# Attention with expert dispatch on one core: row sums spread through a DRAM scratch, values turned by VectorE

## The chip, the core and the metric

The kernel runs on one core of a Trainium2 chip. A core has five engines with an instruction queue each: TensorE (PE, matrix products into PSUM), VectorE (DVE), ScalarE (ACT), GpSimd (POOL) and SyncE (SP, which here only issues DMAs). DMAs run on 16 DMA engines; SP, ScalarE and GpSimd each have a queue to them. Engines wait for each other by semaphores, and each does its own instructions in order. The metric is device time of one execution, in microseconds (us).

## What is computed

`x` and `ctx` are 16 × 256 × 512 numbers. The first half is attention over channels cut into heads, with `ctx` both as keys and as values; the second sends each of 4096 rows to 2 of 8 experts. The reference, cut:

```python
def _L0_xcond_ref(q, k, v, k_length):
    ...
    s = SCALE * jnp.log(k_length.astype(jnp.float32))[:, None, None, None]
    attn = jnp.einsum('bhdq,bhdk->bhqk', qh, kh)
    attn = jax.nn.softmax(s * attn, axis=-1)
    out = jnp.einsum('bhqk,bhdk->bhdq', attn, vh)
...
x = x + _L0_xcond_ref(_layernorm(x, axis=-1), ctx_2048, ctx_2048, itok_B_779_1933)
x = x + _L0_ffn_ref(_layernorm(x, axis=-1), L0_ffn_Wg, L0_ffn_w1, L0_ffn_w2)
```

There are 8 heads of 32 dimensions per batch entry, and 512 queries and 512 keys per head. The experts' layer takes a softmax over 8 logits, the top 2 with a capacity of 1280 rows per expert, two matrix products with a relu between, and adds the results with their gates.

## The kernel before

The function `attention_and_dispatch` makes the first half and writes rows for the experts; the rest of the program, the experts' two products, is not touched by the change.

Work goes by groups: a group is 128 rows of `x`, that is 4 heads × 32 dimensions, with 512 columns. There are 32 groups. A loop over **slots** s does in one slot the scores of group s, the exponentials and weighted sums of group s − 2 and s − 3, the division by the row sums of group s − 4, the logits of group s − 5, and the preparation of group s + 2. Each slot has four **steps** c = 0 to 3 (128 queries or keys each), and each step four **turns** i. The order of every engine is written out by hand in this loop; an edit at `(c, i) == (1, 1)` stands in turn 1 of step 1. Odd slots from 7 on also choose experts for a pair of groups (`pair_in`), which adds small VectorE instructions; GpSimd sends the chosen rows to DRAM in the slot after.

In one turn TensorE makes a score block (L1086, into one of three banks `ps_s`), of which VectorE takes the row maximum (L678), and a turned score block of an earlier group (L1037, into one of three banks `ps_t`) with the maximum subtracted inside the product, of which ScalarE takes the exponential (L460, into `probs`). At the end of a step TensorE adds the weighted sums of the values (L1007, into `ps_o`) and the row sums (L1013, into `ps_l`). Banks are handed out in the order of use: the table made by `bank_turns` numbers each use, and a use waits until the one three before it on the same ring is free (`s_bank`, `t_bank`).

Queries and keys are split into a high and a low part (`khi` by ScalarE at L452, `klo` by GpSimd at L406, `qhi`, `qlo`), and SP copies these into the stacks `kst` and `qst` two slots ahead (L291, L296). SP's order in a slot is: eight small transfers of the row maxima (L251), `xt` and `ct`, `xres`, the store of a result, three copies into `kst`, three into `qst`.

**Values.** The weighted sum needs the values with keys over partitions. TensorE turns `ct` by four transposes at turn 1 of step 2 (`values`, L1051, behind the four of `row_turned`, L1044), into a bank of `ps_t`; ScalarE copies the bank to `vt` (L467).

**Row sums.** `ps_l` holds each row sum in every partition of its head. ScalarE copies `ps_o` and `ps_l` at the end of step 0 (L475, L537) and loads one row per head into 64 partitions (`l_wide`, L541). VectorE takes the reciprocal there (L730) and splits it in two parts (L734, L736). ScalarE loads these as 8 rows (`r_rows`, L521), and TensorE spreads them over all partitions by a product with a 0/1 matrix into a bank of `ps_s` (`shares`, L1059, turn 1 of step 1). VectorE multiplies `o_sb` by that bank (L795); GpSimd adds `xres` (`residual`, L336), VectorE takes the statistics of the sum in step 3 (L695). The last three groups are divided in another way, without this path.

The stage ends with the last two groups and the dispatch of the last rows, and then the experts' products begin. Times in this text count from the first instruction.

## Time and profile before

| what | value |
|---|---|
| median of 3 runs | 2180.99 us (2179.78 to 2181.63) |
| profiled execution, its span | 2177.8 us |
| its granted TensorE clock, mean | 0.995 |
| TensorE busy | 2117.0 us, 97% |
| VectorE / ScalarE / GpSimd busy | 1008.1 / 712.9 / 470.4 us |
| stage of slots, 54 to 615 us: TensorE busy | 556.75 of 561 us |
| the same: VectorE, ScalarE, DMA share | 441.56 us, 358.73 us, 0.71 |
| end of the dispatch, 615 to 677 us: TensorE busy | 55.29 of 62 us |
| experts, 677 to 2177.8 us: TensorE busy | 1483.54 of 1500.8 us |

The profile is of one execution; the median of the runs lies 3.2 us above its span. A busy share is an average, and a matmul that is followed by a wait is drawn longer than it is, so a share near 1 does not tell that an engine never waited. The DMA share is the mean over 16 DMA engines.

### The profile page before, as it was taken

To read this page: it belongs to the slowest core of one execution; us is meant where nothing else is said; L and a number is where in the kernel's file an instruction comes from. 1 tells how busy PE (TensorE), PEld (TensorE's weight loads), DVE (VectorE), ACT (ScalarE), POOL (GpSimd) and SP (SyncE) were. 2 spreads that over 40 slices of the span, in tenths; PEclk is the share of its full clock that TensorE was granted. 3 is DMA by queue.
4 is the path that set the end of the run, shared out by engine and by line. 5 is a ranking of instruction groups with operands and counts; after the bars stand their busy time and mean duration, and the time that the engine had idled before them with its cause. 6 is when DMAs were issued, how large, how long until landed. Compare 5 with 4: busy or idle time off the path is not lost. (4 is left out here: it accounts for less than half of the span.)

```text
span 2177.8 us, 27085 instructions
## 1 busy us (share of the span) xinstructions
PE 2117.0 (97%) x10179; PEld 1518.8 (70%) x10179; DVE 1008.1 (46%) x1908; ACT 712.9 (33%) x1216; POOL 470.4 (22%) x593
## 2 busy tenths in 40 slices
PE   3999999999999999999999999999999999999997
PEld 1445454455547888878888887888888788888776
DVE  5677878878765434234324423423432342343211
ACT  1666666666652222113212212311311231132110
POOL 3334444343422111110301201031030102101101
PEclk9999999999999999999999999999999999999999
DMA  9876767776635435212613612422441252241101
GB/s 147 160 165 157 181 157 188 168 187 162 146 114 161 115 70 132 58 22 85 131 20 78 150 26 58 125 50 43 114 98 25 56 134 52 48 125 31 16 6 20
DMA packets 183895, 216.61 MB, mean 99 GB/s; under 512 B 39731, under 2 KB 111419, under 8 KB 183740
## 3 DMA queue, kind: packets, MB, share of 16 engines
q1 hardware_dynamic: 154128, 173.21, 34.1%
q0 software_dynamic: 22240, 37.92, 9.1%
q10 hardware_dynamic: 7372, 3.42, 0.7%
q8 instruction: 97, 1.59, 0.3%
q14 instruction: 58, 0.48, 0.1%
HBM read 113.93 MB, written 68.29 MB: 84 GB/s over the span
## 5 line engine op out<-in xcount | busy, mean ns | idle before, releaser
L1590 DVE SCALAR_TENSOR_TENSOR hlo<-ps_h,hhi 128x512 fp32r<-128x512 f32 x256 | 177.0, 692 | 928.4 <-ACT hhi L1467 928.4
L1467 ACT ACTIVATE hhi<-ps_h 128x512 fp32r<-128x512 f32 x256 | 152.9, 597 | 1123.4 <-PE ps_h L1731 1123.4
L1729 PE MATMUL ps_h<-xhi,w1hi 128*128 128x512 f32 x1024 | 404.9, 395 | 2.5 <-PEq L1316 1.3
L1748 PE MATMUL ps_y<-w2hi,hhi 128*128 128x512 f32 x1024 | 404.7, 395 | 0.7 <-DVE hlo L1590 0.7
L1749 PE MATMUL ps_y<-w2lo,hhi 128*128 128x512 f32 x1024 | 403.0, 394 | 1.0 <-issue 1.0
L1750 PE MATMUL ps_y<-w2hi,hlo 128*128 128x512 f32 x1024 | 403.7, 394 | 0.0
L1731 PE MATMUL ps_h<-xhi,w1lo 128*128 128x512 f32 x1024 | 403.6, 394 | 0.0
L1730 PE MATMUL ps_h<-xlo,w1hi 128*128 128x512 f32 x1024 | 403.0, 394 | 0.0
L678 DVE TENSOR_REDUCE nmax<-ps_s 128x1 f32<-128x512 f32 x512 | 335.7, 681 | 128.5 <-PE ps_s L1086 124.6
L460 ACT ACTIVATE probs<-ps_t 128x512 f32<-128x512 f32 x504 | 273.0, 604 | 183.1 <-PE ps_t L1037 145.8
L1729 PEld LDWEIGHTS ps_h<-xhi,w1hi 128*128 128x128 f32 x1024 | 192.3, 188 | 48.5 <-issue 3.9
L1749 PEld LDWEIGHTS ps_y<-w2lo,hhi 128*128 128x128 f32 x1024 | 193.1, 189 | 46.7 <-issue 1.5
L1730 PEld LDWEIGHTS ps_h<-xlo,w1hi 128*128 128x128 f32 x1024 | 193.0, 188 | 45.2
L1748 PEld LDWEIGHTS ps_y<-w2hi,hhi 128*128 128x128 f32 x1024 | 192.3, 188 | 46.0 <-DVE hlo L1590 1.1
L1731 PEld LDWEIGHTS ps_h<-xhi,w1lo 128*128 128x128 f32 x1024 | 192.3, 188 | 45.8
L1750 PEld LDWEIGHTS ps_y<-w2hi,hlo 128*128 128x128 f32 x1024 | 192.3, 188 | 45.8
L1086 PE MATMUL ps_s<-kst,qst 96*128 96x512 f32 x416 | 192.0, 472 | 30.5 <-DMA qst<-qlo 27.6
L1402 POOL DMA_INDIRECT out_x<-y,ids x64 | 103.3, 1614 | 453.6 <-DVE y L1632 439.0
L1086 PEld LDWEIGHTS ps_s<-kst,qst 96*128 96x128 f32 x416 | 81.7, 197 | 146.8 <-DVE nmax L678 76.7
L1037 PE MATMUL ps_t<-qst,kst 98*128 98x512 f32 x408 | 164.0, 406 | 1.9 <-DMA qst<-nturn 1.2
L1384 POOL TENSOR_TENSOR ids<-xtail,zeros 128x4 int32<-128x4 int32 x15 | 4.9, 328 | 712.8 <-DMA xtail<-dispatched 712.8
L1007 PE MATMUL ps_o<-probs,vt 128*32 128x512 f32 x1016 | 137.1, 612 | 3.3 <-ACT probs L460 3.3
(202 smaller groups left out, 2007.2 us busy)
## 6 DMA issues: line engine op xcount, KB each, us to landing
raw<-in_L_ffn_w SPq DMA_DIRECT2D x128, 512.0 KB, 4.9
qst<-qhi SPq DMA_DIRECT2D x64, 256.0 KB, 5.8
xin<-dispatched SPq DMA_DIRECT2D x60, 256.0 KB, 5.8
kst<-khi SPq DMA_DIRECT2D x52, 256.0 KB, 6.4
xt<-in_x SPq DMA_DIRECT2D x32, 256.0 KB, 3.1
ct<-in_ctx SPq DMA_DIRECT2D x32, 256.0 KB, 4.5
qst<-qlo SPq DMA_DIRECT2D x32, 256.0 KB, 6.8
xres<-in_x SPq DMA_DIRECT2D x32, 256.0 KB, 4.7
```

The lines of the kernel that those rows point to most:

```text
L460: nc.scalar.activation(probs[n % 3][:, i, :], t_at(k)[:], ACT.Exp).then_inc(t_free, 1)
L678: nc.vector.tensor_reduce(nmax[s % 2][:, i, c:c + 1], s_at(k)[:], AX, ALU.max, negate=True).then_inc(s_free, 1)
L1037: nc.tensor.matmul(bank[:], kst[g % KR][0:STACK + 2, i, cols], qst[g % KR][0:STACK + 2, i, :], start=True, stop=True).then_inc(t_done, 1)
L1086: nc.tensor.matmul(bank[:], qst[s % KR][0:STACK, c, cols], kst[s % KR][0:STACK, c, :], start=True, stop=True).then_inc(s_done, 1)
L1467: nc.scalar.activation(hhi[k % 2][:], ps_h[k % 3][:], ACT.Relu).then_inc(hhi_ready, 1)
L1590: nc.vector.scalar_tensor_tensor(hlo[k % 2][:], ps_h[k % 3][:], 0.0, hhi[k % 2][:].bitcast(F32), ALU.max, ALU.subtract).then_inc(h_ready, 1)
L1729: nc.tensor.matmul(to, w1hi[:, c, fs], xhi[n % 2][:, c, :], start=(c == 0), stop=False)
L1730: nc.tensor.matmul(to, w1hi[:, c, fs], xlo[n % 2][:, c, :], start=False, stop=False)
L1731: done = nc.tensor.matmul(to, w1lo[:, c, fs], xhi[n % 2][:, c, :], start=False, stop=(c == NC4 - 1))
L1748: nc.tensor.matmul(ps_y[b][:], hhi[k % 2][:, bs], w2hi[:, f, :], start=(f == 0), stop=False)
L1749: nc.tensor.matmul(ps_y[b][:], hhi[k % 2][:, bs], w2lo[:, f, :], start=False, stop=False)
L1750: done = nc.tensor.matmul(ps_y[b][:], hlo[k % 2][:, bs], w2hi[:, f, :], start=False, stop=(f == NF - 1))
```

## The change

It has two parts. **Row sums:** the reciprocals are no longer split. ScalarE stores `r_wide` (64 × 32) to one of two 4 × 512 scratch tensors in DRAM (`shares_out`, where the loads of `r_rows` were), and behind turn 1 of the next step 0 it waits for that store and loads the scratch back with each of its 4 rows repeated for 32 partitions (`shares_in`, into `r_all`, 128 × 512). VectorE multiplies `o_sb` by `r_all` at turn 3 of step 1 (`weighed`); TensorE's product and its bank go. **Values:** SP loads a second copy of the values (`values_in`, four loads of 32 partitions) with blocks of 32 × 32 in place, and VectorE turns each block at turn 1 of step 2 (`values_turned`); TensorE's transposes, their bank and ScalarE's copy go. For this the keys stand in another order in `khi` and `klo` (`by_block`, `by_chunk`).

```diff
@@ bank_turns: the turns "vt" and "r" go
-                if i == 1 and c == 2 and live(s - 1):
-                    t_turn["vt", s - 1] = len(t_turn) + 1
...
-                if i == 1 and c == 1 and live(s - 4):
-                    s_turn["r", s - 4] = len(s_turn) + 1
...
+    shares = [nc.dram_tensor(f"shares{i}", (HPG, D), F32, kind="Internal").ap() for i in range(2)]
...
-        vt = [sb(f"vt{i}", [P, NC4, P]) for i in range(4)]
+        vsq = [sb(f"vsq{i}", [P, HPG, NC4, Q]) for i in range(2)]
+        vt = [sb(f"vt{i}", [P, HPG, NC4, Q]) for i in range(4)]
...
+        r_wide = [sb(f"r_wide{i}", [HPG * LW, D // LW]) for i in range(2)]
+        r_all = [sb(f"r_all{i}", [P, D]) for i in range(2)]
...
+        def by_block(tile):
+            return tile[:].rearrange("p (b c r) -> p c b r", b=NC4, c=NC4)
+        def by_chunk(tile):
+            return tile[:].rearrange("p (c b r) -> p c b r", b=NC4, c=NC4)
...
+            def values_in(g):
+                if g >= 2:
+                    sp.wait_ge(vt_made, g - 1)
+                for b in range(NC4):
+                    sp.dma_start(vsq[g % 2][Q * b:Q * b + Q].rearrange("j h c r -> j h (c r)"),
+                                 ctx_rows[g * P:g * P + P, P * b:P * b + P].rearrange("(h j) r -> j h r", h=HPG)
+                                 ).then_inc(vsq_ld[g % 2], 16)
...
+                if live(s):
+                    values_in(s)
                 if live(s - 3):
                     rows_in(s - 3)
...
             def residual(g):
-                pool.wait_ge(s_free, s_turn["r", g])
+                pool.wait_ge(o_scaled, g + 1)
...
-                    nc.gpsimd.tensor_tensor(klo[g % 2][:], ct[g % 4][:], khi[g % 2][:].bitcast(F32), ALU.subtract
-                                            ).then_inc(klo_ready, 1)
+                    nc.gpsimd.tensor_tensor(by_chunk(klo[g % 2]), by_block(ct[g % 4]),
+                                            by_chunk(khi[g % 2]).bitcast(F32), ALU.subtract).then_inc(klo_ready, 1)
...
-                nc.scalar.activation(khi[g % 2][:], ct[g % 4][:], ACT.Copy).then_inc(khi_ready, 1)
+                nc.scalar.activation(by_chunk(khi[g % 2]), by_block(ct[g % 4]), ACT.Copy).then_inc(khi_ready, 1)
...
+            def shares_out(g):
+                act.wait_ge(r_ready, g + 1)
+                if g >= 2:
+                    act.wait_ge(r_ld[g % 2], 16 * turns(g - 2, 2))
+                act.dma_start(shares[g % 2].rearrange("h (c q) -> (h c) q", c=LW), r_wide[g % 2][:]
+                              ).then_inc(r_st[g % 2], 16)
+            def shares_in(g):
+                act.wait_ge(r_st[g % 2], 16 * turns(g, 2))
+                if g >= 2:
+                    act.wait_ge(o_scaled, g - 1)
+                act.dma_start(r_all[g % 2][:], shares[g % 2].unsqueeze(1).to_broadcast([HPG, HD, D])
+                              ).then_inc(r_ld[g % 2], 16)
...
                         if (c, i) == (3, 0) and live(s - 3):
-                            g = s - 3
-                            act.wait_ge(r_ready, g + 1)
...
+                            shares_out(s - 3)
+                        if (c, i) == (0, 1) and live(s - 4):
+                            shares_in(s - 4)
...
+            def values_turned(g):
+                dve.wait_ge(vsq_ld[g % 2], (16 * NC4) * turns(g, 2))
+                if g >= 4:
+                    dve.wait_ge(pv_done, 4 * (g - 3))
+                nc.vector.transpose(vt[g % 4][:].rearrange("p h c d -> p (h c) d"),
+                                    vsq[g % 2][:].rearrange("p h c r -> p (h c) r")).then_inc(vt_made, 1)
...
+            def weighed(g):
+                if g <= G - 4:
+                    dve.wait_ge(r_ld[g % 2], 16 * turns(g, 2))
+                else:
+                    dve.wait_ge(l_saved, g + 1)
...
+                nc.vector.tensor_tensor(o_sb[g % 2][:], (o_sb[g % 2] if g < G - 1 else ps_o)[:],
+                                        (r_all if g <= G - 4 else l_sb)[g % 2][:], ALU.mult).then_inc(o_scaled, 1)
...
+                        if (c, i) == (2, 1) and live(s - 1):
+                            values_turned(s - 1)
...
+                        if (c, i) == (1, 3) and live(s - 4):
+                            weighed(s - 4)
...
                 if c == 0:
-                    pe.wait_ge(t_free, t_turn["vt", g])
+                    pe.wait_ge(vt_made, g + 1)
```

ScalarE, from step 3 of an even slot into step 0 of an odd one. `probs` are the exponentials, `lexp` those of the logits. Before:

```order
L460 ACTIVATE probs<-ps_t 128x512 x3
L521 DMA r_rows<-r_hl 4x16x32 x2
L460 ACTIVATE probs<-ps_t 128x512 x3
L548 ACTIVATE qhi<-qf 128x512
L460 ACTIVATE probs<-ps_t 128x512 x3
L530 ACTIVATE lexp<-lg,lmax 128x8 x2
L460 ACTIVATE probs<-ps_t 128x512
L475 ACTIVATE o_sb<-ps_o 128x512
L537 ACTIVATE l_sb<-ps_l 128x512
L541 DMA l_wide<-l_sb 64x1x32
```

and now:

```order
L465 ACTIVATE probs<-ps_t 128x512 x3
L477 DMA shares<-r_wide 64x32
L465 ACTIVATE probs<-ps_t 128x512 x3
L551 ACTIVATE qhi<-qf 128x512
L465 ACTIVATE probs<-ps_t 128x512 x2
L484 DMA r_all<-shares 128x1x512
L465 ACTIVATE probs<-ps_t 128x512
L533 ACTIVATE lexp<-lg,lmax 128x8 x2
L465 ACTIVATE probs<-ps_t 128x512
L471 ACTIVATE o_sb<-ps_o 128x512
L540 ACTIVATE l_sb<-ps_l 128x512
L544 DMA l_wide<-l_sb 64x1x32
```

Where two loads of `r_rows` stood there is one store to `shares`; the load of `r_all` stands between the second and the third exponential of step 0, ahead of the copies of `o` and `l`.

VectorE, from turn 0 of step 1 of an even slot to turn 0 of step 3. `nmax` are the maxima (the row with x5 covers turns 2 and 3 of step 1 and turns 0 to 2 of step 2). Before:

```order
L618 STREAM_TRANSPOSE nturn<-nmax_hl 128x128
L597 BN_AGGR st_0<-st_0 128x2
L678 TENSOR_REDUCE nmax<-ps_s 128x1
L795 TENSOR_TENSOR o_sb<-ps_s,o_sb 128x512
L678 TENSOR_REDUCE nmax<-ps_s 128x1 x5
L730 RECIPROCAL r_wide<-l_wide 64x32
L734 CAST r_hl<-r_wide 64x32
L736 TENSOR_TENSOR r_hl<-r_wide,r_hl 64x32
L678 TENSOR_REDUCE nmax<-ps_s 128x1
L603 TENSOR_SCALAR qf<-xt,st_0 128x512
L678 TENSOR_REDUCE nmax<-ps_s 128x1
```

and now:

```order
L616 STREAM_TRANSPOSE nturn<-nmax_hl 128x128
L595 BN_AGGR st_0<-st_0 128x2
L696 TENSOR_REDUCE nmax<-ps_s 128x1 x3
L654 TENSOR_TENSOR o_sb<-o_sb,r_all 128x512
L696 TENSOR_REDUCE nmax<-ps_s 128x1 x2
L622 STREAM_TRANSPOSE vt<-vsq 128x512
L696 TENSOR_REDUCE nmax<-ps_s 128x1
L748 RECIPROCAL r_wide<-l_wide 64x32
L696 TENSOR_REDUCE nmax<-ps_s 128x1
L601 TENSOR_SCALAR qf<-xt,st_0 128x512
L696 TENSOR_REDUCE nmax<-ps_s 128x1
```

The product into `o_sb` moved behind the last maximum of step 1 and takes `r_all`; the turning of the values stands ahead of the third maximum of step 2; two small instructions on the reciprocals are gone.

SP in one slot, behind the transfers of the maxima (`xin` stands for one of the five buffers of `kst`). Before:

```order
L271 DMA xt<-in_x 128x1x512
L275 DMA ct<-in_ctx 128x1x512
L258 DMA xres<-in_x 128x512
L262 DMA out_x<-x_0 128x512
L291 DMA xin<-khi 32x4x512
L291 DMA xin<-klo 32x4x512
L291 DMA xin<-khi 32x4x512
L296 DMA qst<-qhi 32x4x512 x2
L296 DMA qst<-qlo 32x4x512
```

and now:

```order
L282 DMA xt<-in_x 128x1x512
L285 DMA ct<-in_ctx 128x1x512
L262 DMA vsq<-in_ctx 32x4x128 x4
L269 DMA xres<-in_x 128x512
L273 DMA out_x<-x_0 128x512
L303 DMA xin<-khi 32x4x512
L303 DMA xin<-klo 32x4x512
L303 DMA xin<-khi 32x4x512
L308 DMA qst<-qhi 32x4x512 x2
L308 DMA qst<-qlo 32x4x512
```

The four loads of `vsq` stand between `ct` and `xres`, ahead of the copies into `kst` and `qst`.

## Rows read from the trace of the kernel before

**Rows 1.** Busy time, TensorE clock, DMA share of an odd and an even slot

```profile
300.17:319.15 18.98, 18.85 (x118) 9.66 (x117) 16.28 (x49) 11.97 (x23) 5.89 (x10) 1.00 0.67 147
319.15:337.76 18.61, 18.61 (x115) 9.14 (x114) 13.93 (x30) 12.23 (x25) 10.13 (x15) 1.00 0.74 189
```

**Rows 2.** Timeline of TensorE, even slot: start, duration, line, tile

```profile
316.17 1.06 PE L1007 MATMUL ps_o<-probs,vt 128*32 128x512 f32 x8
...
319.15 0.50 PE L1059 MATMUL ps_s<-r_rows,to_dims 8*128 8x512 f32 x1
...
321.02 1.07 PE L1007 MATMUL ps_o<-probs,vt 128*32 128x512 f32 x8
...
324.39 0.63 PE L1051 MATMUL ps_t<-ident,ct 128*128 128x128 f32 x4
...
325.32 0.40 PE L1086 MATMUL ps_s<-kst,qst 96*128 96x512 f32 x1
...
325.88 1.07 PE L1007 MATMUL ps_o<-probs,vt 128*32 128x512 f32 x8
```

**Rows 3.** Timeline of TensorE in slot 3

```profile
74.42 1.07 PE L1007 MATMUL ps_o<-probs,vt 128*32 128x512 f32 x8
...
78.88 0.49 PE L1037 MATMUL ps_t<-qst,kst 98*128 98x512 f32 x1 [0.70 <-ACT probs L460]
79.31 1.06 PE L1007 MATMUL ps_o<-probs,vt 128*32 128x512 f32 x8
...
83.67 1.07 PE L1007 MATMUL ps_o<-probs,vt 128*32 128x512 f32 x8
```

**Rows 4.** Timeline of ScalarE, from an odd into an even slot

```profile
309.67 1.26 ACTq L521 DMA_DIRECT2D r_rows<-r_hl  x2
...
314.87 2.06 ACT L460 ACTIVATE probs<-ps_t 128x512 f32<-128x512 f32 x4 [1.38 <-PE ps_t L1037]
318.16 0.60 ACT L475 ACTIVATE o_sb<-ps_o 128x512 f32<-128x512 f32 x1 [1.23 <-PE ps_l L1013]
```

**Rows 5.** Groups by line: busy us, mean ns of one

```profile
L618 DVE STREAM_TRANSPOSE nturn<-nmax_hl 128x128 f32<-128x128 f32 x32 | 9.6, 301 | 0.0
```

**Rows 6.** Timeline of VectorE, then of TensorE, odd slot

```profile
309.37 0.69 DVE L678 TENSOR_REDUCE nmax<-ps_s 128x1 f32<-128x512 f32 x1 [0.19 <-PE ps_s L1086]
...
310.58 0.67 DVE L678 TENSOR_REDUCE nmax<-ps_s 128x1 f32<-128x512 f32 x1
...
311.69 0.39 PE L1086 MATMUL ps_s<-kst,qst 96*128 96x512 f32 x1
```

**Rows 7.** Timeline of TensorE at slot 2; DMA queue, 15 to 55

```profile
52.19 0.79 PE L1086 MATMUL ps_s<-xin,qst 96*128 96x512 f32 x1 [2.59 <-DMA qst<-qlo]
...
q1 hardware_dynamic: 3317, 5.76, 100.9%
```

**Rows 8.** DMA queue: packets, MB, share; 308 to 308.5, then 318 to 320

```profile
q1 hardware_dynamic: 89, 0.17, 91.0%
...
q1 hardware_dynamic: 144, 0.26, 105.9%
```

**Rows 9.** ScalarE's queue: 300.29 to 303.5, 309.67 to 316.5, 87.7 to 96

```profile
q10 hardware_dynamic: 68, 0.01, 1.9%
...
q10 hardware_dynamic: 136, 0.02, 2.5%
...
q10 hardware_dynamic: 424, 0.56, 23.6%
```

**Rows 10.** Timeline of SP's issues, start of an even slot

```profile
314.92 1.45 SPq L296 DMA_DIRECT2D qst<-qhi  x2
```

**Rows 11.** DMA queues: 309.67 to 311, then 312 to 314.5

```profile
q1 hardware_dynamic: 189, 0.35, 82.3%
...
q1 hardware_dynamic: 227, 0.41, 103.4%
q10 hardware_dynamic: 45, 0.01, 3.0%
```

More of the change, by code:

```diff
@@ L90, in bank_turns @@
                         t_turn["x2t", g - 3] = len(t_turn) + 1
-                    if c == 2 and g == G - 2:
-                        t_turn["vt", G - 1] = len(t_turn) + 1
                     if c == 1 and g == G - 1:
@@ L155, in attention_and_dispatch @@
         l_wide = [sb(f"l_wide{i}", [HPG * LW, D // LW]) for i in range(2)]
-        r_wide = sb("r_wide", [HPG * LW, D // LW])
-        r_hl = [sb(f"r_hl{i}", [HPG * LW, 2, D // LW], F32R) for i in range(2)]
-        r_rows = [sb(f"r_rows{i}", [MROWS, D], F32R) for i in range(2)]
-        to_dims = sb("to_dims", [MROWS, P], F32R)
-        dims = sb("dims", [HPG, P])
+        r_wide = [sb(f"r_wide{i}", [HPG * LW, D // LW]) for i in range(2)]
+        r_all = [sb(f"r_all{i}", [P, D]) for i in range(2)]
         x1 = [sb(f"x1_{i}", [P, D]) for i in range(2)]
@@ L379, in _ @@
             for s in range(-2, SLOTS):
-                if s == 0:
-                    nc.gpsimd.memset(dims[:], 0.0).then_inc(dims_made, 1)
-                    pool.wait_ge(dims_made, 1)
-                    dims_hd = dims[:].rearrange("p (h d) -> p h d", h=HPG)
-                    nc.gpsimd.affine_select(out=dims_hd, in_=dims_hd, compare_op=ALU.not_equal, fill=1.0, base=0,
-                                            pattern=[[-1, HPG], [0, HD]], channel_multiplier=1).then_inc(dims_made, 1)
                 if live(s + 2):
@@ L512, in _ @@
                             nc.scalar.activation(x2t[:], t_at(k)[:], ACT.Copy).then_inc(t_free, 1)
-                        if i == 1 and c == 2 and live(s - 1):
-                            values(s - 1)
                         if (c, i) == (3, 0) and live(s - 3):
-                            g = s - 3
-                            act.wait_ge(r_ready, g + 1)
-                            if g >= 2:
-                                act.wait_ge(s_done, s_turn["r", g - 2])
-                            for part in range(2):
-                                act.dma_start(r_rows[g % 2][HPG * part:HPG * part + HPG, :].bitcast(F32
-                                              ).rearrange("h (c q) -> h c q", c=LW),
-                                              r_hl[g % 2][:, part, :].bitcast(F32)).then_inc(r_ld[g % 2], 16)
+                            shares_out(s - 3)
+                        if (c, i) == (0, 1) and live(s - 4):
+                            shares_in(s - 4)
                         if (c, i) == (0, 2) and pair_in(s):
@@ L548, in _ @@
                         nc.scalar.activation(qhi[g % 2][:], qf[:], ACT.Copy).then_inc(qhi_ready, 1)
-                if s == 0:
-                    act.wait_ge(dims_made, 2)
-                    for part in range(2):
-                        act.dma_start(to_dims[HPG * part:HPG * part + HPG, :].bitcast(F32), dims[:]).then_inc(dims_st, 16)
                 if 1 <= s <= FILLS // 2:
@@ L562, in _ @@
                     powers(g, c, 0)
+                    if g == G - 2 and c == 0:
+                        shares_in(G - 4)
                     powers(g, c, 1)
@@ L566, in _ @@
                         row_turned(g - 3)
-                    if g == G - 2 and c == 2:
-                        values(G - 1)
                     if g == G - 1 and c == 1:
@@ L1006, in weighted @@
                     hd = slice(HD * h, HD * h + HD)
-                    nc.tensor.matmul(ps_o[hd, :], vt[g % 4][:, c, hd], probs[n % 3][:, h, :],
+                    nc.tensor.matmul(ps_o[hd, :], vt[g % 4][:, h, c, :], probs[n % 3][:, h, :],
                                      start=(c == 0), stop=(c == NC4 - 1))
@@ L1025, in last_weighted @@
                     hd = slice(HD * h, HD * h + HD)
[L1026 removed]
+                    done = nc.tensor.matmul(ps_o[hd, :], vt[(G - 1) % 4][:, h, NC4 - 1, :], held[:, h, :],
                                             start=False, stop=True)
@@ L1045, in row_turned @@
                 done.then_inc(t_done, 1)
-            def values(g):
-                pe.wait_ge(c_ld[g % 4], 16 * turns(g, 4))
-                bank = t_bank(t_turn["vt", g])
-                for q in range(NC4):
-                    done = nc.tensor.transpose(bank[:, P * q:P * q + P], ct[g % 4][:, P * q:P * q + P], ident[:])
-                done.then_inc(t_done, 1)
-            def shares(g):
-                pe.wait_ge(r_ld[g % 2], 32 * turns(g, 2))
-                if g == 0:
-                    pe.wait_ge(dims_st, 32)
-                bank = s_bank(s_turn["r", g])
-                nc.tensor.matmul(bank[:], to_dims[:], r_rows[g % 2][:], start=True, stop=True).then_inc(s_done, 1)
             def logits(g):
@@ L1091, in _ @@
                             row_turned(s - 5)
-                        if i == 1 and c == 2 and live(s - 1):
-                            values(s - 1)
                         if i == 1 and c == 3 and (live(s - 5) or pair_in(s)):
@@ L1111, in _ @@
                             done.then_inc(s_done, 1)
-                        if i == 1 and c == 1 and live(s - 4):
-                            shares(s - 4)
                     if c == 0 and live(s - 3):
@@ L1127, in _ @@
                     turned_logits(g, c, 1)
-                    if g == G - 2 and c == 0:
-                        shares(G - 4)
                     weighted(g if c else g - 1, (c - 1) % NC4)
@@ L1135, in _ @@
                             logits(G - 5)
-                        if c == 2:
-                            values(G - 1)
                         if c == 3:
```

65 lines of the change are left out of this document (16 added, 49 removed).

## Prediction

> **What bounds the kernel now.** I first read the busy time of two neighbouring slots of the attention stage [rows 1]. The reader is to see TensorE busy for 18.85 of 18.98 us and 18.61 of 18.61, VectorE for 16.28 and 13.93, and the DMA engines at 0.67 and 0.74. So TensorE looks like the bound, and less work on it would shorten each slot. That share hides waits, though: where a matmul waits, the one before it is drawn longer. So I next read TensorE's own order in time, step by step. A step runs from one start of L1007 to the next [rows 2, 3].
>
> The change touches two steps. Step 2 holds the four transposes of the values (L1051) behind the four of x2. It lasts 325.88 − 321.02 = 4.86 [rows 2], and 83.67 − 79.31 = 4.36 in slot 3, which has the value transposes alone [rows 3]. One block of four thus costs about 0.49. Step 1 holds the matmul of the row sums (L1059) and lasts 321.02 − 316.17 = 4.85 [rows 2]. But slot 3 runs this step without that matmul, and takes 79.31 − 74.42 = 4.89 [rows 3]: its last turned score (78.88) waits for ScalarE. By the code ScalarE must copy o and l out of PSUM, wait for that copy and issue the load of l_wide before it reaches the exponential that frees that bank. Step 1 is bounded by ScalarE, not by what TensorE does in it.
>
> **What the change takes off the path.** Values: 0.49 us in step 2 of slots 2 to 31, 30 × 0.49 = 14.7 us. Slot 1 gains nothing: its end is set by DMA. Row-sum matmul: nothing in 28 main slots, by the comparison of 4.85 with 4.89. For odd slots, a wait in slot 4 and the tail's pair of blocks I put in 2 us together (bounds 0 and 28 × 0.50, that matmul's duration [rows 2]); I stay near zero because slot 3 is the nearest row. ScalarE loses the copy of the values and VectorE two small instructions; neither sets a step where these stand, so I count nothing.
>
> **What it adds beside other work.** VectorE turns 128x512 values in squares of 32. Its one transpose here has 128 columns and takes 301 ns [rows 5]; a maximum over 512 columns takes 0.69 us [rows 6]. Bounds: 0.70 as such a pass, 1.20 as four transposes. I take 0.70, as the fixed part of four instructions would be paid once. In even slots VectorE has room (13.93 of 18.61). In odd slots the new instruction stands ahead of the maximum of turn (2,2); from there to the maximum at 309.37 VectorE idled 0.19 us, and the next maximum that TensorE needs, started at 310.58, ended at 311.25 against a score wanted at 311.69 [rows 6]. That score now wants to start 0.49 earlier, at 311.20, and VectorE is pushed by 0.2 to 0.7 net of the two instructions that go and the idle time: a loss of 0.2 (0.70) to 0.7 (1.20) in 13 odd slots. I take 0.2, so 2.6 us; the range holds 9. The product o × r moves from turn (1,1) to (1,3), reads SBUF in place of PSUM, and costs as before. The strided reads in the high and low parts of the keys (ScalarE, GpSimd) lie ahead of a transfer needed two slots later; even at twice their time that slack covers them.
>
> SP issues four more loads a slot, of 32 partitions each. They stand behind the eight maxima transfers and ahead of the copies into kst and qst, which have most of a slot to spare; only at the start have they none. From 15 to 55 us SP's queue fills the engines (100.9%), and the scores of slot 2 wait for qst at 52.19 [rows 7]. The first value load lies in that queue ahead of it. 256 KB cost 0.7 us as a load over 128 partitions (89 packets of 2 KB in 0.5 us) and 2 us as a copy into 32 (144 packets in 2 us) [rows 8]. I take 1.5.
>
> **What it adds on the path.** The reciprocals now go to DRAM and come back over all 128 partitions (r_all, 256 KB) by a load that ScalarE issues after turn (0,1). VectorE waits for it in order, in front of the maximum of (2,0); behind it TensorE's score (2,3) waits, as there are three banks. When must it land? In an even slot that score starts at 325.32 [rows 2], so it wants 324.83 after the change. Ahead of it stand the product and one maximum, 0.69 each [rows 6], which makes 323.4. ScalarE can issue at 315.4, behind the second of four exponentials that start at 314.87 [rows 4]. That leaves 8.0 us.
>
> How long does it take? The packets tell how a transfer is spread. The two loads of r_rows and two fills together show 424 packets, r_rows alone 136, l_wide 68 [rows 9]. A fill has 128 rows, so 288 is 2 × (128 + 16); l_wide and each r_rows have 64, and 68 is 64 + 4: one closing packet for each engine used. l_wide's source begins with 4 rows, and it gets 4 engines. r_all's source begins with the 4 rows of the scratch. So I expect 4 engines with 32 + 1 packets each, where a fill has 16 with 8 + 1.
>
> By the Trainium skill (DMA: Bandwidth & Descriptors, section "Why a DMA increments its semaphore by 16 and not by 1") the engine count is the largest up to 16 that divides the outermost sizes of both sides, and a leading small dimension confines a DMA. By that rule r_all gets 4 engines; no run here shows such a broadcast, and with 16 engines the time would be that of the first rival below.
>
> A 2 KB packet out of DRAM takes 0.5 × 0.91 × 16 / 89 = 0.082 us of an engine; a copy into 32 partitions 2 × 1.06 × 16 / 144 = 0.235 [rows 8]. Alone, r_all would need 33 × 0.082 = 2.7 us. It is not alone: SP issues the three copies into qst from 314.92 on [rows 10], 24 packets per engine. The engines alternate: from 312 to 314.5 r_rows moved 45 packets on its 4 engines (11 each) while SP moved 227 on 16 (14 each) [rows 11]. About 1.5 us pass before a first packet (r_rows was issued at 309.67; up to 311 SP's queue has all traffic [rows 4, 11]), and 0.4 to the wait's end, both estimates. Landing thus takes 1.5 + 2.7 + 0.4 = 4.6 us with no sharing, 10.2 with all 24 copy packets between. I take 18 of 24 in an even slot, as the copies lead by half a microsecond: 8.8, 0.8 late. In an odd slot the dispatched rows are in the queues too, so 10.2; VectorE has no reserve there, so lateness counts from about 7.3: 2.9 late. Each stall gives the copies ahead of the next load more time to drain, so I halve both: 0.4 and 1.5, a mean of 1.0 over 28 slots, 28 us. In slots 4 to 6 r_all also queues behind two fills on ScalarE's queue: 1.5 each, 4.5 us.
>
> Sum: −14.7 − 2 + 2.6 + 1.5 + 28 + 4.5 = +19.9 on a span of 2177.8, so 2197.7. The median of the runs lies 3.2 above that span (2180.99), so **2201 us**.
>
> **Rivals.** First, faster: r_all lands inside 8 us everywhere, because it gets 16 engines or overtakes the copies. Then 28 and 4.5 go: 2180.99 − 12.6 = 2168. For it: the 4.6 us of an unshared transfer. Against it: engine counts and the alternation [rows 9, 11]. Second, far slower: no relief, every copy packet lies between, and dispatch traffic adds 2 us in odd slots. Stalls of 2.2 and 4.7, 3.5 × 28 = 98, fills 9: 2181 − 12.6 + 107 = 2275. For it: a loaded queue in all of the window. Third, ScalarE as the new bound: it stands still in front of r_all's issue until the store to DRAM has landed, with exponentials and the copy of o behind it. The store is issued at 309.67 [rows 4], so it has 5.7 us, and ScalarE's idle 1.2 ahead of L475 on top; from 6.9 on, each microsecond costs 28 us. At 8 us that is 31 more than the forecast: 2232. Against it: the store is spread over 64 rows, and r_rows, on 4 engines, moved all its packets inside 6.8 us [rows 9]. The Trainium skill says on the same page (section "Anatomy of one DMA", for GpSimd's path) that a DMA's fixed cost of about 2 us is mostly the receipt of its last write, and heaviest for HBM. By that rule the store would land later than r_rows did; no row here times a small store.
>
> **How the numbers follow.** Forecast 0.45 (its own range 2182 to 2230), first rival 0.27, second 0.20, third 0.08. The range takes in the first rival and reaches to near the second: 2164 to 2262. A measurement of this kernel tells 0.2% (4.4 us) from no change. Faster by that: the first rival but for its upper edge, 0.25. Within it: that edge and the forecast's low end, 0.10. Slower: 0.65.
>
> **What would show it.** In the trace after: step 2 about 0.49 shorter wherever VectorE does not wait, and step 1 still near 4.85; the transpose of the values near 0.70; idle time of VectorE ahead of the product o × r, put down to r_all, of some 3 us where TensorE loses 1, and TensorE's wait for a maximum at the last score of step 2; ScalarE's queue with 132 packets for r_all. Wrong would be: no wait for r_all (first rival), a wait of ScalarE's third exponential for the store (third), or step 1 shorter by 0.4, which would mean that the matmul was on the path after all.

## The result, and the profile after

The kernel before takes 2181.31 us (median of 6 runs, 2179.24 to 2184.70), the changed one 2269.01 us (median of 6, 2251.80 to 2273.07). The ratio on record is 1.0368, with a 95% interval of 1.0336 to 1.0400: slower (the two medians alone give 1.0402). The forecast was 2201 us in a range of 2164 to 2262. The side was right, and so was the chain of waits; the time lies above the range, and the loss is more than four times the one forecast. Of all executions told of below one, of sums_21, was slow (9065.15 us at a granted clock of 0.223); its median takes it in, its ratio does not. The profiled execution of the changed kernel is the quickest of its six: its span is 2250.1 us, 72.3 more than that of before.

All of it is in the stage of slots. Step lengths, from one start of the weighted values (L1007 before, L999 after) to the next, as medians over slots 6 to 30:

| | step 0 | step 1 | step 2 | step 3 |
|---|---|---|---|---|
| even slots, before | 3.93 | 4.86 | 4.87 | 4.99 |
| even slots, after | 3.93 | 4.83 | 6.38 | 4.99 |
| odd slots, before | 3.93 | 4.93 | 4.86 | 5.26 |
| odd slots, after | 3.93 | 4.84 | 7.10 | 6.14 |

Step 1 did not move, though its matmul is gone. Step 2, which should have been 0.49 shorter, is 1.5 and 2.2 longer, and step 3 of odd slots 0.9. The timeline of the changed kernel through steps 1 and 2 of an even slot (start, duration, engine, line; in brackets the idle time before and what ended it) shows why:

```profile
308.44 0.55 ACTq L484 DMA_DIRECT2D r_all<-shares  x1
...
309.21 1.06 PE L999 MATMUL ps_o<-probs,vt 128*32 128x512 f32 x8
...
314.05 1.07 PE L999 MATMUL ps_o<-probs,vt 128*32 128x512 f32 x8
...
318.41 0.69 DVE L654 TENSOR_TENSOR o_sb<-o_sb,r_all 128x512 f32<-128x512 f32 x1 [3.79 <-DMA r_all<-shares]
...
319.76 0.50 PE L1064 MATMUL ps_s<-kst,qst 96*128 96x512 f32 x1 [1.75 <-DVE nmax L696]
...
320.22 0.70 DVE L622 STREAM_TRANSPOSE vt<-vsq 128x512 f32<-128x512 f32 x1
...
320.43 1.06 PE L999 MATMUL ps_o<-probs,vt 128*32 128x512 f32 x8
```

The load of r_all is issued at 308.44, and the product that needs it starts at 318.41, 9.97 us later. VectorE stood still for 3.79 of them, and TensorE's last score of step 2 for 1.75, waiting for a maximum behind the product. Before, the same score started at 325.32 without a wait [rows 2]. The groups by line (busy us, mean ns, then the idle time before) say that this is the rule, and give the price of the transpose:

```profile
L654 DVE TENSOR_TENSOR o_sb<-o_sb,r_all 128x512 f32<-128x512 f32 x29 | 20.0, 690 | 108.3 <-DMA r_all<-shares 108.3
...
L622 DVE STREAM_TRANSPOSE vt<-vsq 128x512 f32<-128x512 f32 x32 | 22.5, 702 | 0.0
```

VectorE waited 108.3 us in all for r_all, in 27 slots, 4.0 each. The transpose of the values takes 702 ns, close to the 0.69 us of a maximum over 512 columns [rows 6] and far from four times the 301 ns of one over 128 [rows 5]. TensorE's waits from 90 to 660 us (in total, times, longest) give what reached the path, and one of ScalarE's stands below them:

```profile
PE ps_s L1064 <- DVE nmax L696: 52.0, 25, 4.7
PE ps_t L1029 <- ACT probs L465: 20.4, 27, 1.5
...
ACT probs L465 <- DMA shares<-r_wide: 9.2, 6, 2.2
```

The 52.0 us are the stall. (The 20.4 lie in step 1, whose median did not change.) In six slots ScalarE's exponential stood until the store to the scratch had landed. In three of these, slots 4, 11 and 21, step 1 is 0.66, 1.06 and 0.45 longer than before. How did the load travel? ScalarE's queue in the changed kernel (packets, MB, share of 16 engines) from 310 to 312, 312 to 314, 314 to 316, 316 to 317 and 317 to 318, with SP's queue under the first and the last, and at the end ScalarE's queue from 315 to 316 alone:

```profile
q10 hardware_dynamic: 30, 0.06, 25.8%
...
q1 hardware_dynamic: 109, 0.19, 79.7%
...
q10 hardware_dynamic: 29, 0.06, 25.5%
...
q10 hardware_dynamic: 25, 0.05, 26.2%
...
q10 hardware_dynamic: 42, 0.09, 25.6%
...
q10 hardware_dynamic: 6, 0.00, 1.5%
...
q1 hardware_dynamic: 32, 0.06, 21.0%
...
q10 hardware_dynamic: 10, 0.02, 23.7%
```

The first five rows of ScalarE's queue sum to 132 packets, which is 4 × (32 + 1), and 25 to 26% is four engines of sixteen, busy throughout. So r_all has 4 engines, as [rows 9] had it for other loads from four rows. By the Trainium skill (DMA: Bandwidth & Descriptors, section "Why a DMA increments its semaphore by 16 and not by 1") a leading dimension of 4 gives that; the trace agrees. But r_all does not alternate evenly with the copies, as I read [rows 11]: the copies have 79.7%, about the other 12.8 engines, and r_all its own nearly to itself. SP's queue moves nothing from 315 to 317; the 32 packets that follow in the next microsecond, on 21.0% or some 3.4 engines, belong to the rest of the copies, which stood on r_all's engines until it had ended. From 310 to 316 a packet costs 6 × 4 / 84 = 0.29 us of an engine, from 316 to 317 it costs 4 / 42 = 0.095. The copies beside it are not the whole reason: from 315 to 316, when none of them moves, a packet costs 4 / 10 = 0.4. What slows it there is open.

One loss was in no step of the prediction. In another slot TensorE waits 1.96 us, and the eight matmuls behind take 1.94 us in place of the usual 1.06 (timeline, then the windows of one microsecond, whose column before the last two is the granted clock):

```profile
233.11 0.80 PE L1064 MATMUL ps_s<-kst,qst 96*128 96x512 f32 x1 [1.96 <-DVE nmax L696]
...
234.26 1.94 PE L999 MATMUL ps_o<-probs,vt 128*32 128x512 f32 x8
```

```profile
231.00:232.00 1.00, 0.15 (x1) 0.00 (x0) 0.24 (x1) 0.86 (x2) 0.00 (x0) 1.00 0.25 59
232.00:233.00 1.00, 0.00 (x0) 0.00 (x0) 1.00 (x3) 0.00 (x0) 0.47 (x1) 0.91 0.57 80
233.00:234.00 1.00, 0.89 (x2) 0.50 (x2) 1.00 (x3) 0.00 (x0) 0.95 (x2) 0.50 0.83 271
234.00:235.00 1.00, 1.00 (x5) 0.20 (x8) 1.00 (x3) 0.60 (x1) 0.26 (x1) 0.50 0.80 259
235.00:236.00 1.00, 1.00 (x12) 0.23 (x8) 1.00 (x3) 0.00 (x0) 0.84 (x1) 0.50 0.89 219
236.00:237.00 1.00, 1.00 (x12) 0.17 (x4) 0.09 (x1) 0.00 (x0) 0.85 (x1) 0.88 0.76 139
```

After the idle 2 us the granted clock is 0.50, the lower level of 1.2 GHz, for some 3.3 us of work. This is not so behind every stall: twelve of the 25 have such a stretch behind them, two of these only after some 6 us, and the stall of 1.75 us in the first timeline has none. Over windows of two microseconds from 90 us to the end of the slots, the sum of length × (1 − granted clock) is 23.9 us here; before, the clock was 1.00 in both slots of [rows 1] and the same sum is 0. The four slowest of the six runs had granted clocks of 0.976 to 0.979 over the whole time, the profiled one 0.984; time × (1 − clock) makes that some 13 of the 17 us by which the median lies above the profiled run, an estimate.

So of the 72.3 us, as an estimate: 52 of stalls, 24 of low clock (part of it inside the stalls, so the two overlap), 5 of VectorE's longer work (step 3 is 0.4 longer in odd slots 7, 17, 21 and 23, where the clock stayed full), 2 of ScalarE's waits for the store, and −13 for the values. The start adds 5: step 0 of slot 4 begins at 92.47 in place of 87.58, behind waits for qst and 10 us at 1.2 GHz in slot 3. Behind the slots 3 come back. That makes 72.

### The profile page after: what moved, and what is told of

Its sections match the earlier page's. It is cut to its first block and busy times, and to the rows that moved or that the text cites. A ratio compares the mean times of both kernels' runs of the same rounds, so it can differ in the third digit from the quotient of the medians.

```text
span 2250.1 us, 26747 instructions
## 1 busy us (share of the span) xinstructions
PE 2111.8 (94%) x10022; PEld 1499.8 (67%) x10022; DVE 1009.2 (45%) x1882; ACT 691.7 (31%) x1184; POOL 470.7 (21%) x591
## 5 line engine op out<-in xcount | busy, mean ns | idle before, releaser
L465 ACT ACTIVATE probs<-ps_t 128x512 f32<-128x512 f32 x505 | 280.3, 599 | 283.4 <-PE ps_t L1029 244.0
L999 PE MATMUL ps_o<-probs,vt 128*32 128x512 f32 x1016 | 145.5, 647 | 3.4 <-ACT probs L465 3.4
```

The costliest lines, as they stand in the source:

```text
L465: nc.scalar.activation(probs[n % 3][:, i, :], t_at(k)[:], ACT.Exp).then_inc(t_free, 1)
```

## The experiments

Seventeen kernels, told by the question that each answers. Kernels that were timed together share their runs of before, whose medians lay between 2184.3 and 2187.7 us.

**One part at a time.** shares_only takes over the row sums alone, values_only the values alone; the diffs are the two halves of the change's.

> Only the row sums go by DRAM; the values stay on TensorE, as before. Theory (the load of r_all is late by itself: 4 engines, alternating with the copies into qst): VectorE's product still starts about 10 us after the load is issued, TensorE waits at the last score of step 2, and where it waits long its granted clock falls. It lacks the gain of the values (15 us) and has 0.49 us more work in step 2, so each wait is that much shorter: 2225 to 2255 us. Rival (the value loads on SP's queue make r_all late): r_all lands inside 8 us, 2175 to 2190.

> Only the values are loaded in squares and turned by VectorE; the row sums stay as before. Theory: step 2 is 0.49 us shorter in 30 slots (14.7), VectorE takes back some 3 and the start of the stage up to 7: 2168 to 2176 us. Rival (the value loads or the longer work of VectorE are what made the changed kernel slow): 2200 or more, with step 2 not under 4.86.

shares_only: 2238.12 us, ratio 1.0245 (1.0222 to 1.0267). VectorE waits 98.3 us for r_all in 27 slots with no value load in sight. The row sums alone make most of the loss, as the theory had it. values_only: 2191.29, ratio 1.0026 (1.0007 to 1.0044), and between the two expectations. Step 2 is 4.37 in all its slots, the 0.49 that was forecast; but step 3 of odd slots is 5.84 in place of 5.26, in some slots steps 3 and 0 are up to 2.5 longer, and 13.7 us of clock are lost.

**The product later.** The changed kernel with VectorE's product three turns on:

```diff
-                        if (c, i) == (1, 3) and live(s - 4):
+                        if (c, i) == (2, 2) and live(s - 4):
                             weighed(s - 4)
```

> The changed kernel, with the product o x r_all three turns later, after the maximum of turn (2,2) instead of (1,3). Theory (the only loss is VectorE's stand for r_all): the load may now land some 3.5 us later, 11.5 us after its issue, which 25 of 28 did: 2165 to 2185 us, the granted clock back at about 0.995. Rival (the DMA traffic itself slows the copies and so TensorE): still over 2220.

2271.77, ratio 1.0404 (1.0378 to 1.0430): the theory missed, and the time is in the rival's range. The product no longer waits at all and step 2 is back at 4.37, but a wait has come up one instruction ahead, at the reciprocal in front of the product (its idle time, us, times, in this kernel):

```profile
  DMA l_wide<-l_sb: 40.9, 13
```

l_wide comes from four rows too, so it has 4 engines, on the same queue as r_all and behind it. In the changed kernel VectorE's stand for r_all hid that. Step 3 of odd slots is 10.15 here, TensorE waits 32.0 us for maxima in 11 turns, and 49.5 us of clock are lost.

**Order or engines?** load_first lets SP issue r_all between the copies into kst and qst; four_first does the same with four loads, one per head, each with 32 partitions.

```diff
+                    if live(s - 3):
+                        shares_in(s - 3)          # on SP
                     sp.wait_ge(qhi_ready, g + 1)
...
-                sp.dma_start(r_all[g % 2][:], shares[g % 2].unsqueeze(1).to_broadcast([HPG, HD, D])
+                for h in range(HPG):              # four_first
+                    sp.dma_start(r_all[g % 2][HD * h:HD * h + HD], shares[g % 2][h:h + 1].to_broadcast([HD, D])
```

> The changed kernel, with the load of r_all issued by SP between the copies into kst and those into qst, so that it stands ahead of the qst copies in the same queue; still 4 engines. Theory (alternating with the qst copies costs the time): it lands 6 to 7 us after its issue at about the same moment, VectorE waits little: 2165 to 2195 us. Rival (33 packets on 4 engines are too slow whatever stands beside them): a lag of 9 us or more and over 2240.

> As load_first (SP issues r_all ahead of the copies into qst), but as four loads of 32 partitions, one per head, so that each spreads over 16 engines: 8 rows and one closing packet or less on each engine in place of 33 on each of 4. Theory (the 4 engines make r_all late, wherever it stands): the product starts 5 to 7 us after the first of the four issues, against 10.3 in load_first, and VectorE's wait of 5.5 us a slot shrinks to 1 to 2.5; 2195 to 2250 us, as SP still waits for the store and the four issues take 2 us. Rival (the way from DRAM is slow, or the copies hold it back on any engines): still 9 us or more and over 2290 us.

load_first: 2321.31, ratio 1.0618 (1.0585 to 1.0651), the rival. The product still starts 9.6 to 10.7 us after the issue; standing ahead of the copies does not help a load on 4 engines. VectorE's idle time before the product, and below it that of four_first and of four_loads (which comes next):

```profile
  DMA r_all<-shares: 155.3, 27
```

```profile
  DMA r_all<-shares: 17.3, 15
```

```profile
  DMA r_all<-shares: 79.3, 25
```

four_first: 2190.29, ratio 1.0020 (1.0002 to 1.0038), below its range. Only the spread of the load differs in the code, and 131 us go: in this place the 4 engines are what costs. The 131 us are more than the load's own time, though. The product starts 7.2 to 10.5 us after the first issue, which is not the 5 to 7 expected, and the issue itself comes 4.5 us after that of the store (median) in place of 7.5, since the store that SP stands for lands sooner (2.9 us after its issue in place of 7.5, medians of the landings that the traces have). four_loads, run later, spreads the load in its own place on ScalarE:

> The changed kernel with r_all as four loads of 32 partitions in its own place, on ScalarE's queue after turn (0,1): three more issues of 0.55 us on ScalarE. Theory (16 engines in place of 4 end most of VectorE's wait): the product starts 7 to 8 us after the first issue, but ScalarE's 1.65 us lengthen step 0 or 1: 2195 to 2235 us. Rival (the copies issued at the same moment are what holds r_all back): a lag of 9.5 us and more, 2260 or more.

2242.23, ratio 1.0267 (1.0243 to 1.0291). The wait falls from 108.3 us to 79.3, in 25 slots; step 1 is 5.25 in even slots and 6.12 in odd ones (medians), and the last of the four loads is issued 1.3 to 2.7 us after the first. The direction is the theory's, the time worse than its range. So neither the spread alone (27 us off the changed kernel) nor the place alone (load_first, 52 us on top of it) ends the wait; both together do. What holds back 16 engines in the load's own place, the copies or the later issues, no run tells apart.

**Is the clock part of it?** more_work lets TensorE do the four transposes of x2 twice ahead of the score that waits:

```diff
-                for q in range(NC4):
+                for q in range(2 * NC4):
+                    q = q % NC4
```

> The changed kernel, with the four transposes of x2 in step 2 done twice (the second overwrites the first with the same), so TensorE has 0.49 us more to do ahead of the score that waits, in 28 slots. Theory (part of the loss is not the wait but the clock that falls to 1.2 GHz after TensorE has stood still): the wait shrinks by what the work adds, so the slot is no longer, and the clock falls less often: 2235 to 2268 us, with a mean granted clock above 0.984. Rival (the waits alone are the loss, the low clock a minor matter): the same time where VectorE waits and up to 14 us more elsewhere, 2268 to 2283 us, the clock unchanged.

2254.91, ratio 1.0350 (1.0324 to 1.0375). The time is in the theory's range. 14 us of work cost nothing: they vanish in the wait. The loss of clock is 20.5 us against 23.9, and the stall 42.9 against 52.0. The interval overlaps that of the changed kernel, so this run does not separate the clock's share by time; that share stands on the windows alone.

**Why the values alone gain nothing.** values_later moves the transpose of the values; sums_later also the reciprocal and r_rows; values_unloaded is values_later without most of the value loads.

```diff
-                        if (c, i) == (2, 1) and live(s - 1):        # values_later
+                        if (c, i) == (3, 3) and live(s - 1):
                             values_turned(s - 1)
...
-                        if (c, i) == (2, 2) and live(s - 3):        # sums_later, reciprocal
+                        if (c, i) == (3, 1) and live(s - 3):
...
-                if live(s):                                          # values_unloaded
+                if live(s) and s < 2:
                     values_in(s)
```

> Only the values by VectorE, as in values_only, with its transpose moved from turn (2,1) to the end of the slot (after the maximum of (3,3)), where VectorE has idle time; the values are first needed a step later than that. Theory (in odd slots the 0.70 us pushed VectorE's maxima and step 3 grew from 5.26 to 5.83): step 3 of odd slots is back at 5.26, so odd slots last 18.4 instead of 18.97, and fewer waits let the clock fall: 2164 to 2178 us. Rival (the value loads, through the copies, set what values_only lost): no change from 2191.

> As values_later, with VectorE's reciprocal (and the two small instructions behind it) moved from turn (2,2) to (3,1), and ScalarE's issue of r_rows from (3,0) to (3,2). Theory (what is left over in values_later is VectorE waiting for l_wide, 8 times in the stage, up to 2.7 us each, and TensorE's clock at 1.2 GHz behind each): l_wide may land 3.6 us later, the waits go, slots are 18.2 and 18.4 throughout: 2162 to 2172 us. Rival (the lost time comes from the DMA load in some other way): 2180 or more.

> As values_later, but the value loads are issued for the first two groups only; later groups turn those again, so the output is not the reference's. It leaves out 30 x 4 loads, 7.7 MB. Theory (the value loads fill the queues, and so l_wide lands late): VectorE's waits for l_wide go, 2160 to 2170 us. Rival (step 2 is shorter, so l_wide is wanted earlier, whatever the loads do): the waits stay, 2180 or more.

values_later: 2187.03, ratio 1.0011 (1.0001 to 1.0020); a miss in time. Step 3 of odd slots is back at 5.28, as the theory said. From slot 6 to 30, eight of the 13 even slots last 18.2 and four of the 12 odd ones 18.5 or 18.6, some half a microsecond less than before. The others are longer: nine times VectorE's reciprocal waits for l_wide, 10.3 us in all. One of them (timeline of values_later, then the window behind it):

```profile
344.71 1.06 PE L1020 MATMUL ps_o<-probs,vt 128*32 128x512 f32 x8
...
348.37 0.34 DVE L740 RECIPROCAL r_wide<-l_wide 64x32 f32<-64x32 f32 x1 [2.67 <-DMA l_wide<-l_sb]
...
349.80 0.40 PE L1104 MATMUL ps_s<-picked,earlier 128*128 128x16 f32 x2 [2.04 <-DVE nmax L688]
...
353.19 1.08 PE L1020 MATMUL ps_o<-probs,vt 128*32 128x512 f32 x4
```

```profile
352.00:353.00 1.00, 0.96 (x2) 0.50 (x2) 0.83 (x5) 0.50 (x1) 0.00 (x0) 0.50 1.12 201
```

l_wide is 2.67 us late, TensorE stands 2.04, the clock falls, and this step 3 takes 8.48 in place of 5.26. In values_unloaded no reciprocal waits, and 12 of the 13 even slots last 18.2, six of the 12 odd ones 18.5: the value loads make l_wide late. (Its whole time, 2198.67, tells nothing, since other values route the tokens otherwise; its slots end 8.8 us before those of the kernel before.) sums_later: 2206.90, ratio 1.0100 (1.0075 to 1.0125), a miss. The waits for l_wide are gone, and TensorE waits for r_rows instead, 22.6 us in 17 slots: what was moved later now lands too late.

**What bounds step 1?** sums_load_late is the kernel before with the issue of l_wide moved behind two exponentials:

```diff
+                        if (c, i) == (1, 1) and live(s - 3):
+                            ...
+                            act.dma_start(l_wide[g % 2][:], ...
```

> The kernel before, with one move: ScalarE issues the load of l_wide after the exponential of turn (1,1) and not ahead of that of (1,0). Theory (step 1 is bounded by ScalarE, not by the matmul of the row sums): step 1 goes from 4.85 to 4.3 to 4.5, 28 slots of 0.35 to 0.55: 2165 to 2172 us. Rival (the matmul of the row sums bounds step 1): 4.85 stays, 2181 us.

2180.43, ratio 0.9986 (0.9973 to 0.9999), a miss; step 1 is 4.93 in odd slots and 4.70 in even ones. ScalarE is not the only bound. In the timeline of an odd slot of sums_load_late, VectorE has no gap from 260 us on, and TensorE's score at 261.85 starts when the maximum before it ends:

```profile
260.58 0.49 PE L1061 MATMUL ps_s<-r_rows,to_dims 8*128 8x512 f32 x1
...
261.13 0.66 DVE L680 TENSOR_REDUCE nmax<-ps_s 128x1 f32<-128x512 f32 x1
...
261.85 0.50 PE L1088 MATMUL ps_s<-kst,qst 96*128 96x512 f32 x1
...
262.12 0.69 DVE L797 TENSOR_TENSOR o_sb<-ps_s,o_sb 128x512 f32<-128x512 f32 x1
```

The matmul of the row sums takes one of the three banks that scores go through, and VectorE's product has to empty it. So step 1 has two bounds of nearly one length; the change takes away the one, this run the other.

**Both bounds taken away.** all_moved joins everything: four_first, the transpose at (3,3), l_wide issued after (1,1), reciprocal at (3,1), store at (3,2), product at (2,2). all_unloaded is all_moved with two groups' value loads only. sums_moved has the row sums alone in that form (reciprocal at (2,3), store at (3,1)).

> Both parts of the change, each as the runs so far suggest: r_all as four loads by SP (four_first), the transpose of the values at the end of the slot, l_wide issued after the exponential of (1,1), the reciprocal at (3,1), its store at (3,2), and the product at (2,2). Theory (each of the waits that were found goes, and step 1 loses the matmul and the issue that bounded it): step 2 4.37, step 1 4.4 to 4.6: 2148 to 2170 us. Rival (the longer way of the shares takes the place: SP, standing for the store, brings qst late, or the product's late turn holds up what follows): 2180 or more.

> As all_moved, with the value loads issued for the first two groups only (later groups turn those again, so the output is not the reference's, and the routing that follows from it differs). Read is the stage of slots alone. Theory (the value loads are what holds back step 0 of the odd slots in all_moved): step 0 goes from 5.6 back to 3.93 there and the stage is 25 us shorter than all_moved's. Rival (the order of the moved instructions does it): step 0 stays at 5.6.

> Only the row sums by DRAM (values on TensorE as before), with r_all as four loads by SP ahead of the copies into qst, l_wide issued after the exponential of (1,1), the reciprocal at (2,3), its store at (3,1) and the product at (2,2). Theory (step 1 has two bounds of nearly the same size, TensorE's matmul with VectorE's product behind it, and ScalarE with the issue of l_wide ahead of its exponentials; only when both are moved does it get shorter): step 1 near 4.05 as in all_moved, in 28 slots, no value loads to bring l_wide late: 2155 to 2172 us. Rival (SP's stand for the store, or the four issues, bring qst late or let something else wait): 2180 or more.

all_moved: 2179.90, ratio 0.9984 (0.9964 to 1.0005). sums_moved: 2178.84, ratio 0.9973 (0.9958 to 0.9988). Both miss their ranges. Step 1 is 4.05 in both, as the two bounds have it: 0.8 less than before, in all but a few slots. But step 0 of odd slots went from 3.93 to 5.6, in sums_moved without any value load, and in all_unloaded too (5.7): the theory there fell. (all_unloaded as a whole took 2195.74, which tells as little as that of values_unloaded.) In sums_moved at such a place GpSimd is still dispatching rows when the step begins:

```profile
256.38 0.97 POOL L350 DMA_INDIRECT dispatched<-xrow,rowi  x1 [0.30 <-issue]
...
258.33 0.69 DVE L689 TENSOR_REDUCE nmax<-ps_s 128x1 f32<-128x512 f32 x1 [3.28 <-PE ps_s L1061]
...
259.08 0.50 PE L1061 MATMUL ps_s<-kst,qst 96*128 96x512 f32 x1 [1.34 <-DVE nmax L689]
```

By the code GpSimd's residual waits for the product, and its dispatch stands behind the residual. sums_20 and sums_21 therefore move only the product, to (2,0) and (2,1), and the store back to (3,0).

> As sums_moved, with the store at (3,0) again and the product two turns earlier, at (2,0). Theory (in sums_moved the late product makes GpSimd's residual and its dispatch late, and step 0 of the odd slots pays for it with 1.7 us): step 0 is 3.93 in all slots, r_all costs VectorE up to 1 us in some: 2158 to 2172 us. Rival (the loads of r_all or SP's stand for the store hold back step 0): 5.6 stays, 2176 or more.

> As sums_20, with the product at (2,1), so that r_all has one turn more. Theory: between the two, GpSimd's work 1.2 us later than in sums_20 and less waiting for r_all: 2158 to 2175 us. Rival as there: 2176 or more.

sums_20: 2154.61 us, ratio 0.9868 (0.9841 to 0.9895). sums_21: 2163.51, ratio 0.9898 (0.9870 to 0.9926). Step 0 of odd slots is 3.93 with the product at (2,0), 4.64 at (2,1), 5.62 at (2,2), where the store too stands a turn later. Between the first two only the product's place differs, so that place sets it; why TensorE's results reach the other engines late while GpSimd dispatches is not settled. Steps 0, 1 and 2 of sums_20:

```profile
282.61 1.06 PE L989 MATMUL ps_o<-probs,vt 128*32 128x512 f32 x8
...
286.55 1.06 PE L989 MATMUL ps_o<-probs,vt 128*32 128x512 f32 x8
...
290.60 1.06 PE L989 MATMUL ps_o<-probs,vt 128*32 128x512 f32 x8
...
295.46 1.06 PE L989 MATMUL ps_o<-probs,vt 128*32 128x512 f32 x8
```

3.94, 4.05 and 4.86, VectorE waits nowhere for r_all, and the sum of lost clock is 0. Its span is 23.9 us shorter than that of before. This version beats both kernels. The last run puts the values by VectorE on top:

> sums_20 with the values by VectorE at the end of the slot as well. Theory (both parts gain once nothing waits; but the value loads bring l_wide late, as in values_later): step 2 at 4.37 in place of 4.86, 14 us, less some slots in which VectorE waits for l_wide or r_all and the clock falls: 2143 to 2165 us. Rival (the value loads cost more than step 2 gives, also here): over 2165 us.

2191.72, ratio 1.0031 (1.0015 to 1.0046): the rival. Step 2 is 4.37, but VectorE's reciprocal waits for l_wide 18.0 us in 9 slots (and 7.2 more in 3 that the profile gives no cause for), and 28.9 us of clock are lost. The values gain 0.49 a slot and lose more, wherever they were tried; an earlier place for their loads was not.

## Why the prediction was wrong

Right were the place and the chain: r_all on 4 engines with 132 packets, landing after VectorE wants it, VectorE idle 4 us where TensorE loses 2, the last score of step 2 as the one that waits. Right as well: the 0.49 of the values, the 0.70 of their transpose, the strided reads at no cost (648 ns after against 646 before for ScalarE, 1273 against 1275 for GpSimd), and no gain in step 1. The third rival came in small: the store lands 4.8 us after its issue (median, at most 6.5), and ScalarE stood for it in six slots, 9.2 us in all, of which some 2 reached the path, not 31.

Wrong was the term of 28 us for r_all's lateness, where the stalls measured 52.0; and the low clock, some 24 us more, had no term at all.

- **The landing: 8.8 us forecast, 10.0 measured.** The packets took what was forecast: from 310 to 317, 7.0 us against 6.9, though for another reason (slow packets on engines of its own, not the turns with the copies that I read in [rows 11]), so that agreement is luck. The first came some 1.8 us after the issue, where I gave 1.5, and I gave 0.4 us from the last packet to the end of the wait; it was 0.9 to 1.4 (last packets between 317.0 and 317.5, product at 318.41).
- **The halving.** "Each stall gives the copies ahead of the next load more time to drain, so I halve both: 0.4 and 1.5." It does not: a stall moves the copies along with the load. In 13 of 27 slots the first copy is issued half a microsecond ahead of it, and there the product starts 9.3 to 12.9 us after the load's issue (median 10.1). Only in six slots do the copies lead by 1.5 to 2.2 us, and there it starts after 7.9 to 9.5. Without the halving the recorded terms give (0.8 + 2.9) / 2 × 28 = 51.8 us, and the stalls measured 52.0. That it fits so closely is luck: the even slots lost 2.0, not 0.8. With 10.0 against the deadline of 8.0, an even slot loses 2.0, as measured (6.38 − 4.37); the deadline was right.
- **The clock.** No term for it. Behind twelve of the 25 stalls TensorE worked some 3 us or more at 1.2 GHz; 24 us in all. The trace of before held a hint: after the wait of 2.59 us in [rows 7] the matmuls take 0.63 us in place of 0.40 up to 61 us, though the clock column says 1.00 there, and I read that row for its wait alone.

The second rival (2275) came nearest in time, and its "no relief" was the right half; its stalls of 2.2 and 4.7 (98 us; by its own terms, 10.2 + 2 − 7.3, the second is 4.9) were too long, and the clock made up for it. Of the smaller terms, VectorE's push in odd slots was 0.57, not 0.2, in values_only: 7.4 us in 13 slots, inside the bounds of 2.6 to 9; in the changed kernel it was 0.4. The start, forecast at 1.5, cannot be told: step 0 of slot 4 begins 4.9 us later than before in the changed kernel, but 0.9 and 0.5 us later in values_only and values_later with the same loads. The 4.5 us for the fills did not show: in slots 4 to 6 the product starts 7.9, 9.5 and 10.1 us after r_all's issue, no later than elsewhere.

The 2 us for the matmul were right by a reason that was half of it. I put step 1 down to ScalarE alone; two bounds stood side by side, and the 0.8 us behind both, 22 us in the stage, is the gain that the change's idea held.

## What to carry to other kernels

Before a small transfer is put on the path, count its engines: the loads here that begin with a dimension of four ran on four. Splitting r_all by destination (four loads of 32 partitions) was worth 131 us ahead of the copies, but 27 us in its own place, so try spread and place together. Price a stall of TensorE twice, once as the wait and once as the low clock that may come behind it. And where taking work out of a step gains nothing, look for a second bound of the same length before giving the idea up.

## What the runs showed of the hardware

A 2 KB packet from DRAM cost an engine 0.083 us with none of SP's copies beside it (in the tail, 24 packets in half a microsecond on 4 engines), but 0.27 us while copies ran on the other twelve (59 packets from 310 to 314) and 0.4 us right behind them (10 packets from 315 to 316). On the four engines of r_all the rest of the copies came only when it had ended (SP's queue moves no packet from 315 to 317 and 32 in the microsecond behind). A load issued ahead of those copies in the same queue (load_first) was not faster for it. The cost of the low clock is in no fixed ratio to the waits: in the changed kernel stalls of 52.0 us went with 23.9 us of lost clock; in sums_moved step 0 lost 1.7 us in most odd slots, TensorE waited 17.5 us for maxima, and 5.1 us of clock were lost; in both_20 TensorE waited 16.7 us (9.3 for maxima, 7.4 with no cause given), and 28.9 us of clock were lost.
